# The last attention of an eight-layer chain: a batch's work spread over four steps in place of three, and its products laid out anew in PSUM

## The reference

```
# att3, for each of 8 batches: modality1 = _layernorm(x), modality2 = the context
x1 = layernorm(modality1, ln1_g, ln1_b)      # 256 x 128
x2 = layernorm(modality2, ln2_g, ln2_b)      # 256 x 96
q = x1 @ Wq + bq
k = x2 @ Wk + bk
v = x2 @ Wv + bv
scores = jnp.einsum('bqe,bke->bqk', q, k) * scaling
attn = jax.nn.softmax(scores, axis=-1)
ctx = jnp.einsum('bqk,bke->bqe', attn, v)
return ctx @ Wo + bo                          # added to x
```

## Time and profile before

| | |
|---|---|
| median of three runs | 785.33 us (781.67 to 785.69) |
| span of the profiled execution | 779.4 us |
| last attention, first product of step 0 to first product of `moe3` | 596.78 to 660.15 us of the span |
| PE busy over the span | 638.1 us (82%) |
| DVE, ACT, POOL busy | 490.8, 386.3, 302.9 us |

### The profile page before, as it was taken

The page is one execution under the profiler, slowest core; times in us unless marked ns, Lnnn a source line. Parts: engine busy times, 40 slices in busy tenths (PEclk is TensorE's granted clock), DMA queues, the critical chain, the costliest instruction groups (busy, mean ns, idle before and its releaser), DMA issues.

```text
span 779.4 us, 15312 instructions
## 1 busy us (share of the span) xinstructions
PE 638.1 (82%) x4712; PEld 467.2 (60%) x4712; DVE 490.8 (63%) x1428; ACT 386.3 (50%) x860; POOL 302.9 (39%) x456
## 2 busy tenths in 40 slices
PE   2688788889999887899977777748898777699997
PEld 1355666556665544899944555437796566456665
DVE  4678666877778753556867785636657665455443
ACT  5356465466666565466624655335776444232221
POOL 4435355443333036162747644372545730000000
PEclk9999999999999999699976998777999999699999
DMA  6263423333333200144354441012455100223331
GB/s 185 60 158 97 112 73 90 90 94 88 90 95 89 78 19 38 53 130 119 103 138 114 120 128 42 16 41 83 126 143 157 51 11 1 70 69 105 98 95 56
DMA packets 93575, 68.71 MB, mean 88 GB/s; under 512 B 9800, under 2 KB 84424, under 8 KB 93272
## 3 DMA queue, kind: packets, MB, share of 16 engines
q1 hardware_dynamic: 89400, 59.34, 27.4%
q0 software_dynamic: 4096, 8.40, 3.5%
HBM read 30.94 MB, written 14.35 MB: 58 GB/s over the span
## 4 chain that ended last, share of the span: by engine, by line
PE 36%; DVE 8%; issue 6%; DMA 4%; POOL 3%; ACT 3%; SPq 1%; ACTq 0%; DVEq 0%; POOLq 0%
PE ps L2396 7%; PE ps L2406 4%; PE ps L2434 4%; PE ps L2436 4%; PE ps L2447 4%; DVE negmax L975 2%; DMA late<-outputs_moe,placed 2%; PE ps L2111 1%; PE ps L2095 1%; PE ps L2035 1%; PE ps L2390 1%; PE ps L2083 1%; PE ps L2289 1%; POOL gathered L1600 1%; DVE x_sb L1295 1%
## 5 line engine op out<-in xcount | busy, mean ns | idle before, releaser
L975 DVE TENSOR_REDUCE negmax<-ps 128x2 f32<-128x512 f32 x256 | 169.7, 686 | 87.5 <-PE ps L2083 86.8
L1743 ACT ACTIVATE exps<-ps 128x512 f32<-128x512 f32 x256 | 148.6, 598 | 100.7 <-PE ps L2095 99.9
L2083 PE MATMUL ps<-stack 96*128 96x256 bf16 x512 | 102.8, 295 | 26.7 <-DVE negmax L975 23.4
L2095 PE MATMUL ps<-stack 99*128 99x256 bf16 x512 | 100.8, 287 | 19.2 <-DMA stack<-maxt 17.7
L1600 POOL DMA_INDIRECT gathered<-z,placed x64 | 62.4, 975 | 63.3 <-PE ps L2390 28.6
L1618 POOL DMA_INDIRECT late<-outputs_moe,placed x64 | 62.1, 971 | 50.8 <-issue 15.8
L2095 PEld LDWEIGHTS ps<-stack 99*128 99x128 bf16 x512 | 44.2, 102 | 60.2 <-DMA stack<-maxt 24.4
L2083 PEld LDWEIGHTS ps<-stack 96*128 96x128 bf16 x512 | 47.9, 103 | 51.5 <-DVE negmax L975 39.4
L2111 PE MATMUL ps<-exps,values 128*32 128x256 f32 x1024 | 71.9, 398 | 1.3 <-ACT exps L1743 1.0
L1984 ACT ACTIVATE gated<-ps 128x512 f32<-128x512 f32 x36 | 21.5, 597 | 83.1 <-PE ps L2436 83.1
L2406 PE MATMUL ps<-pack_moe,ht 128*128 x368 | 60.1, 288 | 1.3 <-ACT ht L1970 0.8
(11 more groups left out here) (225 smaller groups left out, 1257.4 us busy)
## 6 DMA issues: line engine op xcount, KB each, us to landing
stack<-qk_parts SPq DMA_DIRECT2D x168, 128.0 KB
stack<-weights_t SPq DMA_DIRECT2D x32, 256.0 KB, 3.3
outputs_moe<-y_kept SPq DMA_DIRECT2D x92, 64.0 KB
ht<-gathered SPq DMA_DIRECT2D x44, 128.0 KB, 2.2
pack_moe<-in_moe SPq DMA_DIRECT2D x11, 256.5 KB, 3.9
pack_moe<-in_moe SPq DMA_DIRECT2D x6, 429.5 KB, 4.1
gathered<-y_kept SPq DMA_DIRECT2D x10, 256.0 KB, 3.6
pack_moe<-in_moe SPq DMA_DIRECT2D x1, 1732.0 KB, 7.4
```

Of the source, the lines that this page charges most:

```text
L975: dve.tensor_reduce(negmax_of[b % 2][:, :, h:h + 1].rearrange("p t h -> p (t h)"), ps[:, h % 2, :].rearrange("p (t k) -> p t k", t=2), AX, ...
L1743: nc.scalar.activation(exps[:, i, :], ps[:, 2 + h % 2, :], ACT.Exp, scale=scale)\
L2083: last = pe.matmul(ps[:, h % 2, t * T:(t + 1) * T], st[0:MAXROW, h, 0, t * P:(t + 1) * P], st[0:MAXROW, h, 1, :], start=True, stop=True)
L2095: last = pe.matmul(ps[:, 2 + h % 2, t * T:(t + 1) * T], st[0:MAXROW + 3, h, 1, t * P:(t + 1) * P], st[0:MAXROW + 3, h, 0, :], start=True, ...
```

## The change

A batch's work is spread over four steps. `turn_o`, `copy_ot`, `project_o` and `add_output` are made for batch n = step-3, one step after the average. Scores alternate between banks 2 and 4 (`scores_bank`), and the maximum between two tiles. Values and averages share bank 1 in halves, transposed averages and projections share bank 5; the writes into a shared bank wait until the other half has been read. The context of a chunk goes into `ctxt_sb`, which has room for all of it. All chunks are turned in banks 6 and 7.

The joins move to later steps, and chunks 2 and 3 are no longer prepared ahead: `LATE_STEPS = {4: 2, 6: 3}` says that in step 4 chunk 2, and in step 6 chunk 3, is joined, measured, normalised, turned and copied inside the step that needs it. In such a step each engine first does the work on older batches, then the chunk, then queries, keys, values and scores of the step's own batch.

The normalisation for `moe3` of tiles 0 to 7 moves from steps 6 and 7 to behind the last step. On POOL `add_bias(1)` moves ahead of the reciprocal root of chunk 2, and `add_bias(3)` ahead of that of chunk 3.

```diff
-TURN_BANKS = {"moe1": (4, 4, 0, 1, 5), "moe2": (4, 4, 4, 0, 1, 5), "att3": (6, 0, 0, 0), "moe3": (0, 1, 6, 7)}
+TURN_BANKS = {"moe1": (4, 4, 0, 1, 5), "moe2": (4, 4, 4, 0, 1, 5), "att3": (6, 6, 6, 6), "moe3": (6, 7, 6, 7)}
...
-JOIN_STEPS = {1: (8,), 2: (9, 10, 11), 3: (12,), 4: (13, 14, 15)}
+JOIN_STEPS = {3: (8,), 4: (9, 10, 11), 5: (12, 13), 6: (14, 15)}
+LATE_STEPS = {4: 2, 6: 3}
...
+        def scores_bank(p):
+
+            return 2 + 2 * (p % 2)
...
@@ DVE, single_head
+                def finish_older(step):
+                    d, n = step - 2, step - 3
+                    if valid(n):
+                        add_output(n)
                     if valid(d):
+                        take_sum(d)
                         average(d)
...
+                for step in range(B):
+                    if step == 0:
+                        apply_all(s, 1, GROUPS[s][1])
+                    if step in LATE_STEPS:
+                        finish_older(step)
+                        for t in JOIN_STEPS[step]:
+                            join_outputs("moe2", t)
+                        i = LATE_STEPS[step]
+                        stats_all(s, i, GROUPS[s][i])
+                        apply_all(s, i, GROUPS[s][i])
+                    keep_values(step)
+                    take_max(step)
+                    if step not in LATE_STEPS:
+                        finish_older(step)
+                        for t in JOIN_STEPS.get(step, ()):
+                            join_outputs("moe2", t)
+                    if step >= 3 and 2 * (step - 3) in GROUPS["moe3"][0]:
+                        take_early_stats(step - 3)
+                finish_older(B)
+                apply_all("moe3", 0, GROUPS["moe3"][0])
+                add_output(B - 2)
                 take_sum(B - 1)
                 route_logits("moe3", 0)
                 average(B - 1)
                 route_pick("moe3", 0, (0,))
-                add_output(B - 2)
+                add_output(B - 1)
...
@@ POOL
                         if t == 13:
+                            add_bias(s, 1)
                             make_rstd_all(s, 2, GROUPS[s][2])
-                            add_bias(s, 1)
                     add_bias(s, 2)
+                    add_bias(s, 3)
                     make_rstd_all(s, 3, GROUPS[s][3])
...
@@ ACT, single_head
+                for step in range(B):
+                    if step in LATE_STEPS:
+                        copy_older(step)
+                        take_exp(step - 1)
+                        copy_chunk(LATE_STEPS[step])
+                        copy_queries(step)
+                        continue
+                    copy_queries(step)
+                    copy_older(step)
+                    if step == 1:
+                        copy_chunk(1)
+                    if step:
+                        take_exp(step - 1)
...
@@ PE, single_head
                 def average(d):
                     wait(pe, "pt_ready", s, d)
-                    wait(pe, "v_ready", s, d)
+                    wait(pe, "v_ready", s, d + 1 if d + 2 in LATE_STEPS else d + 2)
                     wait(pe, "o_ready", s, d - 1)
...
+                def find_values(p):
+                    wait(pe, "v_ready", s, p - 1)
+                    wait(pe, "o_ready", s, p - 2 if p in LATE_STEPS else p - 3)
...
+                def score(p):
+                    wait(pe, "qk_ready", s, p)
+                    wait(pe, "p_ready", s, p - 2)
...
+                for step in range(B):
+                    p, d, n = step, step - 2, step - 3
+                    late = step in LATE_STEPS
+                    if not late:
+                        queries_and_keys(p)
+                    if valid(n):
+                        turn_average(n)
                     if valid(d):
                         turn_probs(d)
...
+                    if late:
+                        project(n) if valid(n) else None
+                        average(d)
+                        turn_all(s, [LATE_STEPS[step]])
+                        turn_context(LATE_STEPS[step])
+                        queries_and_keys(p)
+                    find_values(p)
+                    score(p)
                     if p == 1:
...
+                    if not late:
+                        project(n) if valid(n) else None
+                        average(d) if valid(d) else None
+                turn_average(B - 3)
                 turn_probs(B - 2)
+                project(B - 3)
+                average(B - 2)
                 turn_all("moe3", range(2))
-                average(B - 2)
+                turn_average(B - 2)
                 turn_probs(B - 1)
-                turn_average(B - 2)
+                project(B - 2)
                 logits("moe3", 0)
                 average(B - 1)
-                project(B - 2)
                 turn_average(B - 1)
                 project(B - 1)
```

More of the change, by code:

```diff
@@ L2315, in single_head @@
+                    find_values(p)
+                    score(p)
                     if p == 1:
-                        wait(pe, "qk_ready", s, p)
                         turn_all(s, [1])
                         turn_context(1)
-                    if valid(d):
-                        average(d)
-                    wait(pe, "qk_ready", s, p)
-                    wait(pe, "p_ready", s, p - 1)
-                    for t in range(2):
-                        last = pe.matmul(ps[:, 2, t * T:(t + 1) * T], qk[:, 0, t * P:(t + 1) * P], qk[:, 1, :],
-                                         start=True, stop=True)
```

144 lines of the change are left out of this document (58 added, 86 removed).

## The result

The changed kernel takes **802.9 us** (median of four runs, 800.6 to 807.0), beside 785.5 us of the kernel before on the same chip (781.7 to 786.6): a ratio of 1.023 [1.019, 1.027], 17.4 us slower, where 10.5 us were forecast and the range of the time ended at 801. The profiled execution took 801.3 us, 1.8 us more than its span. Times are counted from here on from the first query of step 1 (602.29 after, 599.77 before): up to the turning of the weights it is 81.5 us after and 63.4 us before.

The account below looks back on a forecast made before the run. It took the last attention to be bound by a chain through PE, ACT and DVE. Shorter steps, then serial late chunks, slower clock and longer tail put the weights 10.5 us later: 785.33 + 10.5 = 795.8 us, range 790 to 801.

Parts of the forecast that it names:

- The ordinary step: Last attention, steps without a late chunk: 4.4 us each, 4.1 for steps 2 and 3; steps 5 and 7 save 5.5 us.
- the clock: PE behind the late steps' waits: half speed for part, so queries to scores take 3.9 us, between 3.0 and 4.8.
- Rival (d): Steps 5 and 7: shared banks add waits, so they keep 6.1 us; time 799.2 us, 10%.
- POOL's gate: Step 4: batch 1's output on DVE waits for POOL's bias behind the fetches of tiles 12 and 13, ready at 618.95.
- One chain: Late steps 4 and 6: PE waits 8 to 10 and 5 to 7 us for serial chunk work, released by DVE's normalisation.
- Rival (b): Late steps: joins and statistics lie under PE's and ACT's work, each costing 4.4 + 2.1 us; time 774.4 us, 4%.
- Rival (c): Late steps: each 2.3 us shorter than the lowest clock case, gain and loss cancel; 789.2 us or less, 5%.
- step 5 and step 6's chain: Ordinary step 5 at 4.4 us, then step 6's serial chain to queries and keys at 11.9 us.
- rival (a): PE's clock at its ends: never half, 793.7 us, 15%; always half behind a wait, 798.6 us, 20%.
- the start of the fetches: POOL's fetches of tiles 12 and 13 issue at 613.56 to 618.27, 1.26 us each, no earlier through the change.
- the tail: From step 7's end to the turning of the weights: 16.9 us, against 13.1 before.
- Around the stage: Whole kernel outside the profiled span: the median lies 5.9 us above it, so 785.33 + 10.5 gives 795.8.

Follow-up runs that it names:

- e1_fill: Changed kernel with unread filler products, 19 and 14 of 256 columns, in PE's two long waits of steps 4 and 6: 797.6 us, ratio 1.015.
- e2_bias: Changed kernel with a second bias tile, POOL's bias of batch 1 moved ahead of the fetches of tiles 12 and 13: 801.2 us, ratio 1.020.
- e5_ahead: Changed kernel with DVE and POOL reordered: tiles joined as they land, late chunks' statistics a step earlier, early bias, early moe3 normalisations: 786.7 us, ratio 1.001.
- e10: e6 with tile 14 joined in step 4 instead of 5 and four fillers instead of five in step 6: 823.2 us where before takes 829.2.
- e9: Changed kernel with fillers, early bias of batch 1 and early moe3 normalisations, chunks still in one piece: 830.3 us where before takes 829.2.
- e6: e5_ahead with five unread filler products ahead of each late chunk's transposes: 782.8 us beside 785.5 of the kernel before, ratio 0.996.
- e3_norm: Changed kernel with the eight moe3 normalisations moved on DVE ahead of the last batch's average: 797.8 us, ratio 1.014.

## Why the prediction was right in direction and short in size

**Right.** *The ordinary step.* Forecast 4.1 early and 4.4 later; measured 3.92 for step 2 and 4.3 for step 3 (611.75 to 616.07), and at full clock 4.43 for step 5 to the end of its average (e1_fill, 638.43 to 642.86). In after itself steps 5 and 7 take 5.32 and 5.79 us, outside the 4.2 to 4.7 of the forecast, by the clock (below). Rival (d), that sharing banks adds waits, is out: at full clock the steps got shorter by what PE's work said.

*POOL's gate.* `add_bias(1)` at 618.3 forecast, 621.67 measured, the output of batch 1 released by it (2.72 us of DVE's waiting). e2_bias puts its price at 2.7 us up to the queries of batch 4. The bias of batch 0, 1.22 us of DVE's waiting ahead of it, was not forecast and was not tested alone.

*One chain.* Waits of PE of 8 to 10 and 5 to 7 us forecast, with the normalisation as the releaser; 7.57 and 6.26 measured, with that releaser; the first is short of its range, as PE had stood 1.90 us already. e5_ahead and e10 against e9 show the cause, not only the coincidence: with the chunk's work spread and the bias and tail mended, 15.5 us of the stage go; with little changed but the spreading, beside all three remedies, 8.4. Rival (b) named that case and its condition, the fetches out of the way and joins under other work. It is true of e5 and not of after; yet its time, 774.4, was too low even for e6 (782.8), which pays 11.9 us for a late step where (b) has 6.5. Rival (c), gain and loss cancel, came only with the order of e5.

**Where 7.6 us are missing.** From the first query of step 1 the forecast has 73.9 us to the weights (673.7 - 599.77); 81.5 were measured.

| term of the sum | forecast, us | measured, us | missing |
|---|---|---|---|
| to the queries of batch 4 | 28.5 | 30.09 | 1.6 |
| rest of step 4 | 3.9 | 4.87 | 1.0 |
| step 5 and step 6's chain | 16.3 | 17.95 | 1.6 |
| rest of step 6 | 3.9 | 4.87 | 1.0 |
| step 7 and tail | 21.3 | 23.71 | 2.4 |

The time shows only 7.1 us of miss (802.9 against 795.8), since 2.5 us more ahead of the attention, 0.5 less behind it and 2.7 between spans and medians (below) nearly cancel: that is luck.

The step that failed is the one on **the clock**, where I took 3.9 us, the middle between 3.0 and 4.8, because no row showed how soon full speed returns. The rest of a late step took 4.87 us both times: the full doubling. The Trainium skill (TensorE: Matmul & The Clock Gate, section HAM oscillation) says that each group behind a wait starts cold, and behind the two long waits the trace agrees with the page and not with my middle. In e5_ahead it agrees only in part: behind 2.50 and 2.72 us the transposes are still at full clock, and what comes 2 us later is at half. And I let the doubling end with the late step, and even rival (a) added only 0.5 us for what follows. The next rows were at half clock too: step 5 took 5.32 us up to the end of its average (637.25 to 642.57) and step 7 took 5.79 (660.07 to 665.86), where e1_fill has 4.43 for both, and from the chunk's first transpose to the queries it took 2.83 us both times in place of 2.19. In all that is some 5.2 of the 7.6 us. The tail had a row at half clock as well:

```profile
676.09 1.53 PE L2316 MATMUL ps<-exps 128*128 128x128 f32 x8
```

That row is 1.16 us in the earlier trace rows, and 1.14 in e3_norm, which lacks the wait of 1.78 us ahead of it; but e1_fill, with that row at 1.23, has a tail as long as after's (17.9 us), so no cost of it shows there. Filling the waits returns 6.5 us in the stage and 5.3 in the median, against the 2.1 that the forecast held for the clock (795.8 against 793.7, the lower end of (a)).

The second miss is **the start of the fetches**. POOL's first fetch came 1.35 us behind the first query of step 1, for a DMA, where before it came 0.62 us behind; the whole row of fetches, 1.26 us apart as forecast, is late by this or a little more, 0.85 us at the bias of batch 1 (621.67 - 602.29, against 618.3 - 599.77 in the forecast). That, 0.3 us more in the joins, statistics and normalisation, and the slow transposes make the 1.6 us in the table's first line.

The third is **the tail**: 17.9 us from the end of step 7's average to the weights, 16.9 forecast. Up to the end of the logits the sum holds (10.2 us, 10.5 forecast), and the 2.2 us for the eight normalisations are near what e3_norm gives for moving them, 2.6. What failed is the last term: from the end of the logits to the turning of the weights the forecast took 6.4 us, DVE's choice of experts alone, though before has 7.9 there, and after took 7.7.

**Around the stage.** I set the sum against the span and added 5.9 us for what lies around it. After has 1.8 us there, and so has every other execution on record here within 0.1 us: the profiled execution of before, by the same 1.8 us, was a short one, some 4 us under its median, and that of after 1.6 under its own. That is why the spans differ by 20.1 and the medians by 17.4 us. Most of what I called surroundings was spread between executions, and an error of the same kind sits in every term that was read from one profile.

## What to carry to other kernels

Taking waits out of the engine that bounds a stage moves the bound to the chain that feeds it: cost the *order* on the feeding queues (what stands between the last fetched tile and the first matmul that needs it) before you count the saving, and give each piece of late work to the step in which its data lands. Price a wait of PE, from the size at which your own rows show the clock fall, at its length plus the doubled matmuls behind it, up to the next stretch that a row shows at full speed; here that reached well into the step behind. Put a filler no longer than the wait that it fills. And profile the old kernel twice before you read 2 us from a difference of stages.

## What the runs showed of the hardware

- Behind waits of 2.50 and 2.72 us the granted clock went to 0.50 (1.2 GHz), some 2 us later, for the 4.9 us of queries to scores (e5_ahead). Behind the wait of 1.90 us in after it is 0.50 from 619.00 to 622.00. Behind the wait of 0.85 us for the average ahead of 643.42 the matmuls are at their usual length in both after and e1_fill (0.60 for the four turns, 1.16 for the average). In the tail, where PE has less to do, waits of 0.85 and 0.47 us were enough: the projection behind them, at 675.92 in e3_norm, takes 1.22 us in place of 0.71.
- Products that nobody reads, 19 and 14 of 256 columns, brought the clock back and held it (0.94 on the mean of 624 to 638 us, over a wait of 7.6 us in after), and the median of e1_fill is 5.3 us less; the same in e6_ahead_fill, 5 and 5 products, 3.9 us against e5_ahead, on another chip with the same time of before.
- The unchanged kernel's stage is 63.4 or 65.4 us by the clock behind chunk 2.
- Chips differ more than any edit here: before takes 785.7, 785.5, 829.2 and 784.8 us on four of them. In the profiles from the slow one the 40 us lie ahead of the last attention, whose first query is at 639.01 in e9_three, in place of 599.3.
